# Self-attention's loop over groups of heads, written out with constant waits

## What is computed

```
x = _layernorm(x + _L0_attn_ref(x, ...))      # masked self-attention, 16 heads of 32
x = _layernorm(x + _L0_xattn_ref(x, ctx, ctx, mask, ...))
x = _layernorm(x + _L0_ffn_ref(x, ...))       # 64 experts, 8 per token, and a shared one

def _L0_attn_ref(x, Wq, bq, Wk, bk, Wv, bv, Wo, bo, attn_scale):
    q = (x @ Wq.T + bq).reshape(B, T, H, D)
    k = (x @ Wk.T + bk).reshape(B, T, H, D)
    v = (x @ Wv.T + bv).reshape(B, T, H, D)
    scores = jnp.einsum('bqhd,bkhd->bhqk', q, k) * attn_scale[0]
    mask = _chunk_mask(T, CHUNK)
    scores = jnp.where(mask[None, None], -jnp.inf, scores)
    attn = jax.nn.softmax(scores, axis=-1)
    out = jnp.einsum('bhqk,bkhd->bqhd', attn, v).reshape(B, T, C)
    return out @ Wo.T + bo
```

## Time and profile before

| | us |
|---|---|
| Median of three runs | 3575.05 |
| Lowest and highest | 3569.9, 3582.3 |
| The profiled execution | 3602.69 |
| Its span, first to last instruction | 3600.6 |
| TensorE busy in the span | 3158.3 |
| VectorE busy in the span | 2176.4 |

### The profile page before, as it was taken

The page is one execution under the profiler, slowest core; times in us unless marked ns, Lnnn a source line. Parts: engine busy times, 40 slices in busy tenths (PEclk is TensorE's granted clock), DMA queues, the critical chain, the costliest instruction groups (busy, mean ns, idle before and its releaser), DMA issues. The chain is left out here.

```text
span 3600.6 us, 63650 instructions
## 1 busy us (share of the span) xinstructions
PE 3158.3 (88%) x18557; PEld 2032.8 (56%) x18557; DVE 2176.4 (60%) x4841; ACT 1384.8 (38%) x3155; POOL 1552.0 (43%) x1110
## 2 busy tenths in 40 slices
PE   7998999989899998989797999997988882999990
PEld 4444444444544444444345777775766771888880
DVE  3645546465554645556354888885666663777775
ACT  1443434434354443534322666664000001444441
POOL 3352434424244342434532333332566664566661
PEclk8999989999999999999998999998999996999995
DMA  4122121222203222021273112211221112899996
GB/s 116 44 68 72 33 69 40 68 72 53 73 15 85 56 68 72 21 68 60 87 253 139 59 62 66 62 62 62 62 53 53 53 50 85 240 253 252 248 254 210
DMA packets 189188, 343.99 MB, mean 96 GB/s; under 512 B 36137, under 2 KB 54698, under 8 KB 187946
## 3 DMA queue, kind: packets, MB, share of 16 engines
q1 hardware_dynamic: 132778, 242.51, 23.3%
q0 software_dynamic: 28800, 48.43, 6.0%
q10 hardware_dynamic: 27392, 50.34, 3.8%
HBM read 206.96 MB, written 83.89 MB: 81 GB/s over the span
## 5 line engine op out<-in xcount | busy, mean ns | idle before, releaser
L553 ACT ACTIVATE sa_probs<-sa_s 128x512 f32<-128x512 f32 (+3 forms) x1280 | 614.9, 537 | 740.6 <-PE sa_s L444 410.8
L338 POOL TENSOR_TENSOR sa_both<-sa_probs 128x2048 f32<-128x2048 f32 (+2 forms) x160 | 589.9, 3687 | 683.3 <-PE sa_pv L471 671.7
L410 PE MATMUL sa_w<-sa_parts 96*128 96x512 f32 (+3 forms) x1280 | 516.5, 454 | 114.8 <-DVE sa_pmax L612 36.1
L444 PE MATMUL sa_s<-sa_parts 128*128 128x512 f32 (+3 forms) x1280 | 458.6, 409 | 18.9 <-ACT sa_probs L553 13.6
L616 DVE TENSOR_REDUCE sa_pmax<-sa_w 128x1 f32<-128x512 f32 (+3 forms) x768 | 419.3, 584 | 86.1 <-PE sa_w L410 82.8
L410 PEld LDWEIGHTS sa_w<-sa_parts 96*128 96x128 f32 x1280 | 236.4, 195 | 407.2 <-DVE sa_pmax L612 120.8
L612 DVE CUSTOM_DVE_ANT_0 sa_w<-sa_w,sa_maskS 128x512 f32<-128x512 f32 (+3 forms) x512 | 326.3, 649 | 227.5 <-PE sa_w L410 220.9
L444 PEld LDWEIGHTS sa_s<-sa_parts 128*128 128x128 f32 x1280 | 243.6, 195 | 130.5 <-ACT sa_probs L553 64.4
L1409 POOL DMA_INDIRECT token_and_weight_of_slot<-rt_entry,rt_sl x256 | 254.6, 995 | 144.7 <-issue 74.8
L462 PE MATMUL sa_pv<-sa_probs,sa_values 128*32 128x512 f32 (+3 forms) x2560 | 274.4, 547 | 0.0
L1230 ACT ACTIVATE xa_sm<-xa_sm,xa_nmax 128x154 f32<-128x154 f32 x512 | 208.8, 410 | 72.4 <-DVE xa_nmax L1162 72.4
(11 more groups left out here) (234 smaller groups left out, 5767.6 us busy)
## 6 DMA issues: line engine op xcount, KB each, us to landing
ex_w<-in_w SPq DMA_DIRECT2D x138, 512.0 KB
sa_parts<-early_halves SPq DMA_DIRECT2D x384, 128.0 KB, 2.5
early_xt<-in_xT SPq DMA_DIRECT2D x32, 1024.0 KB, 5.6
scratch_attention_T<-sa_oT SPq DMA_DIRECT2D x32, 256.0 KB, 2.1
on_at<-scratch_attention_T SPq DMA_DIRECT2D x32, 256.0 KB, 3.2
on_xr<-in_x SPq DMA_DIRECT2D x32, 256.0 KB
scratch_x<-on_xn ACTq DMA_DIRECT2D x32, 256.0 KB, 2.1
scratch_x_T<-on_xnT ACTq DMA_DIRECT2D x32, 256.0 KB, 3.3
```

The source lines that it names most:

```text
L338: pool.tensor_tensor(both[:, :, 0:w], probs[:, even, :, 0:w], probs[:, odd, :, 0:w], ALU.add).then_inc(both_ready, 1)
L410: nc.tensor.matmul(ps[:, 0:w], qparts[0:3 * HD, h, q0:q0 + P], kparts[0:3 * HD, h, k0:k0 + w], start=True, stop=True).then_inc(work_ready, 1)
L444: mm = nc.tensor.matmul(ps[:, 0:w], kparts[:, h, kb * P:(kb + 1) * P], qparts[:, h, q0:q0 + w], start=True, stop=not diag)
L553: nc.scalar.activation(probs[:, r % NPB, h, 0:w], sbank[n % NSB][:, 0:w], ACT.Exp).then_inc(exp_done, 1)
```

## The change

The loop is replaced by Python's own, so that all eight groups are written out on all five engines; `it` is a number everywhere, the values of all waits and the DMAs' addresses are constants, and there is no jump inside self-attention. Which pair follows which, and what a pair does, stay as they were. Lines below self-attention's helpers are 4 lower in number.

```diff
@@ -189,18 +189,16 @@
 
         def each_group(eng, body):
 
-            with eng.Fori(0, ITERS - 1) as it:
-                body(it, True)
-            body(ITERS - 1, False)
+            for it in range(ITERS):
+                body(it, it < ITERS - 1)
 
         def each_from_second(eng, pair):
 
-            with eng.Fori(0, ITERS - 1) as it:
+            for it in range(ITERS):
                 for p in range(1, NPAIR):
-                    pair(it, p, True, (it, p - 1))
-                pair(it + 1, 0, True, (it, NPAIR - 1))
-            for p in range(1, NPAIR):
-                pair(ITERS - 1, p, False, (ITERS - 1, p - 1))
+                    pair(it, p, it < ITERS - 1, (it, p - 1))
+                if it < ITERS - 1:
+                    pair(it + 1, 0, True, (it, NPAIR - 1))
 
         @block.sync
         def _(sp):
@@ -230,8 +228,7 @@
                                      halves[HD * h:HD * (h + 1), c % 2, pair, :].bitcast(F32)).then_inc(spread[c], 16)
 
             def store(it, c):
-                g = sp.snap(it % NG) if not isinstance(it, int) else it % NG
-                b = sp.snap(it // NG) if not isinstance(it, int) else it // NG
+                g, b = it % NG, it // NG
                 sp.wait_ge(o_ready, it * NC + (c + 1))
                 apart(sp, passed)
                 sp.dma_start(aT[g, :, ][:, bass.ds(b * SEQ + chunk_q(c) * CH, CH)], oT[:, c % 2]).then_inc(o_stored[c % 2], 16)
@@ -248,8 +245,7 @@
 
             def body(it, more):
                 if more:
-                    b = sp.snap((it + 1) // NG)
-                    next_g = sp.snap((it + 1) % NG)
+                    b, next_g = (it + 1) // NG, (it + 1) % NG
 
                 sp.wait_ge(pv_done, it * NR + NPB)
                 apart(sp, passed)
```

## The result

| | before | after |
|---|---|---|
| Median, us (6 runs each) | 3574.98 | 3557.97 |
| Lowest and highest | 3569.9, 3582.3 | 3555.2, 3561.89 |
| Ratio after to before | | 0.995, 95% interval 0.9939 to 0.9962 |
| The profiled execution | 3602.69 | 3561.89 |
| Its span | 3600.6 | 3560.1 |

The change is 17.0 us faster in the medians (3574.98 - 3557.97), between 14 and 22 us by the interval. The forecast was 3559.0 us in a range of 3546 to 3578. In the runs of this document one execution, of the kernel with the jump's target fetched ahead, took 4450.54 us at a granted clock of 0.64, against 3596.6 to 3607.0 in its eleven others, and is left out.

What follows compares the result with a forecast made beforehand. TensorE, 88% busy, was taken to bound the kernel. Gains of 12.6 us at the loop's turns and 3.5 from constant waits sum to 16.1, taken off the 3575.05 us median: 3559 us, range 3546 to 3578.

Steps and rivals of the forecast that it cites:

- The bound: In self-attention TensorE, busy 88% of the span, bounds the kernel; with the jump gone, VectorE's reciprocal is late next.
- The refetch hidden beside the reciprocal: At the loop's jump back, fetching the target lies beside VectorE's 3.35 us reciprocal, so removing the stop saves about nothing.
- The rival by which every refetch is paid in full: At six jumps back, TensorE's 2.88 us idle each comes off, 17.3 us plus 3.5: 3554 us, chance 0.10.
- Term A: At the six group changes with a jump, 12.6 us gained, the middle of 6.8 and 18.5.
- if every one becomes the exit's: Six group changes, mean 78.23 us, come down to the 75.15 of the one entered by falling through: 18.5 us.
- SyncE at nothing: SyncE's addresses become constants, but its queue waits for TensorE and VectorE at each step: no gain.
- Terms at nothing: SyncE's constant addresses and GpSimd's wait values in self-attention bring no gain; waits for copies add up to 5.8 us.
- Term B: In self-attention's loop, constant instead of computed wait values gain between 1.1 and 6.0 us, middle 3.5.
- the pricing by the 40 us stretch: A full-clock stretch takes 40.19 us in the loop, 39.96 in the last group: 0.57%, giving the 6.0 us upper end.
- the slower rival: Every group change becomes like the 81.49 us one at clock 0.87, six costing 19.6 us more: 3591 us, chance 0.08.
- a later loop lose its place: Code behind self-attention moves; TensorE's returns in a loop over tiles are refetched, up to 41 us more, chance 0.04.
- keep their lengths: In the profile after, the stages behind self-attention take the same length as before.

## Why the prediction was right, and where it was not

**The bound: right.** TensorE is as busy as it was, the "issue" pieces are gone, and what is late next is VectorE's reciprocal, with the same 3.95 us. The rise of that wait by 18.9 us against 16.5 us of "issue" removed is the row that shows it.

**The refetch hidden beside the reciprocal: right, and shown three ways.** Moved to where nothing covers it, a jump of four engines costs 6.9 us. Fetched ahead on TensorE, it saves nothing (1.0000). Taken off TensorE altogether, it saves nothing (1.0009). The rival by which every refetch is paid in full would have needed 2.88 us each. Its page, the Trainium skill's "Runtime: NRT & Kernel Launch" (Instruction fetch mechanics), says that a taken branch whose target is not fetched stops execution. The runs agree with the stop (3.58 us here, up to 7.04 in the moved jump), and show that what it costs depends on what the other engine is doing meanwhile.

**Term A, 12.6 us for the turns: the group changes did become shorter in the profile, the cause was wrong.** The step that failed is "if every one becomes the exit's". The exit differs from the turns in two things at once, no jump and constant waits behind it, and the prediction gave the difference to the first. With the jump gone and the registers kept on TensorE the ratio is 1.0009, and the group changes are as long as ever; with five of six jumps gone on all engines it is 0.9992 and 0.9991, though there the group changes are short. Nor was the exit's 75.15 us a property of the exit: in the unchanged loop's second profile it was 78.12. What the short changes have in common, the exit of the earlier trace rows nearly so (0.49 us), is that TensorE hardly waits for SyncE's copies. The prediction read that two turns of 81.49 and 76.28 us differ "only" in when the short idle pieces fall; they also differ in this wait, 1.31 us against 0.51.

**SyncE at nothing: wrong in the profile.** "Terms at nothing" kept SyncE's cover and the 5.8 us of waiting for copies as they were. Written out, the copies start 7.0 us after the group's last raw copy at six of seven changes, in place of 7.8, and the wait falls to 0.7 us. What that is worth in the median is open: TensorE written out has the whole gain without it.

**Term B, 3.5 us for registers against constants: far too small.** The step that failed is the pricing by the 40 us stretch of the earlier trace rows. The stretch did become 39.97 us as forecast. But it tells of the other engines: where only they are constant, it was 39.94 us, and the time fell by 3.9 us, about term B but not clear of nothing; where only TensorE is constant, it stayed at 40.20, and the time fell by 20.7. TensorE's constants, which no stretch at full clock that the prediction compared gives a price, carry the whole 17 us in the medians: between TensorE written out (0.9942) and the same with registers kept (1.0009) nothing but the registers differs. That the sum of 16.1 came out near 17.0 is in good part luck: neither term had the cause that the runs show, and the exit on which term A was priced took 78.12 us in the second profile.

**How constants on TensorE become 17 us: open.** What the profiles show is where the clock falls. With all waits constant it falls at the same places in every group, on two chips, and so it does with three groups per turn, registers and all, but for the jump and the first group of the second profile; with TensorE's alone constant it stays away from the last chunk in every group; in the other kernels with a loop the places change from group to group. Of the five executions of TensorE written out four lie within 1.3 us, where eleven of the kernel with the jump fetched ahead spread over 10 us and twelve with no jump and registers kept over 28; but the written-out kernel's twelve on the other chip spread over 11.5 too, so the spread alone proves nothing. All this fits a mechanism in which small delays of the sequencer decide where TensorE's short idle pieces fall and how often the clock follows. It was argued, not shown: no profiled execution adds up to the 17 us inside self-attention, and three groups per turn has a self-attention like the written-out program's, a longer rest, and the time of the loop. So part of any of these differences may lie in the later stages, by a cause that was not looked for. Two kernels that would tell weren't tried: SyncE alone written out, and a jump kept on TensorE with constant waits, which needs semaphores that are reset in each turn.

**Not forecast:** the 6.0 us given back in the last chunks, where the fall of the clock has become the rule. It is the slower rival's mechanism in small. The rival itself, all changes like the one of 81.49 us, didn't happen; nor did a later loop lose its place: the returns of the loops over tiles take 208 ns (median) and 234 at most. But the later stages did not all keep their lengths, as was forecast. Besides the routing stage, cross-attention, from its first matmul to the routing stage's first, took 600.7 us after and 597.0 before. It took 597.4 in both kernels on the other chip, so the change alone doesn't decide it.

## What to carry to other kernels

Where a loop's exit is taken as a picture of the loop written out, list all in which it differs from a turn, and try each alone: jump and computed waits go away together, on every engine's program, and here TensorE's jump was worth nothing and its computed waits about what the whole change brought. List the engine that issues the copies as well: here the scatter of a stretch went with its 0.8 us. Where the stage under change gets shorter and the time doesn't, add up the rest of the program. A refetch is priced by what the other engine does during it, and a stall that is covered can be left alone. The larger gain was the wait that stayed after the change, and to take it the in-order DMA queue behind the moved operation had to be moved as well.

## What the runs showed of the hardware that was not expected

- Waits against computed values on TensorE cost about 0.6% of this kernel (0.9942 without them, 1.0009 with them and no jump), though 33 ns operations in about the same number, run for nothing, cost 0.2%, if anything. How is open.
- A loop that goes round without a stop can get one by being made longer: SyncE's next instruction came 0.3 us after its branch with one group per turn and 3.0 us after with three.
- The written-out program is so regular that two chips gave the same seven group changes to within 0.2 us, while its medians there lay 29 us apart (3557.97 and 3586.75).
- Most of a difference between chips can lie in one stage: the routing stage's 1024 matmuls of one kind took 449.3 and 411.6 us in the two profiles at the top. Why was not tried.
- A profiled execution can be the highest or the lowest of its kernel, by 9.5 us above the median (TensorE written out) or 6.0 below it (three groups per turn), which is a third to a half of the effect under study and more.
